# A mixture of experts with a ring of row buffers: freeing a buffer once its rows are turned, weights through another queue, and no store of empty rows

## What is computed

```python
logits = xt @ wg
probs = softmax(logits); idx = argmax(probs)
mask = one_hot(idx, E); locations = cumsum(mask, axis=0) - mask
mask = mask * (locations < C)                       # C = T // E = 512 places per expert, E = 8
exp_out = einsum("ech,efh->ecf", exp_in, W) + b[:, None, :]
x = x + 0.5 * gate * exp_out_of_the_token
```

## Time and profile before

| | |
|---|---|
| median of three runs | 1435.03 us (1433.06 to 1435.62) |
| the profiled execution | 1434.59 us |
| its span, first to last instruction | 1433.3 us |
| mean granted clock of TensorE | 0.911 of full speed |
| busy: PE, DVE, ACT, POOL | 1115.5, 943.4, 827.8, 319.2 us |
| r = 0, first indirect DMA of results starts | 87.33 us |
| r = 1, first indirect DMA of results starts | 947.45 us |

### The profile page before, as it was taken

How to read it: one execution, slowest core, us unless ns; L and a number is a source line. 1 busy time by engine, 2 the same in 40 slices (tenths; PEclk the granted TensorE clock), 3 DMA queues, 4 the chain that set the end, 5 groups by cost and what they waited for, 6 DMA issues and landing times. The chain is left out here.

```text
span 1433.3 us, 30188 instructions
## 1 busy us (share of the span) xinstructions
PE 1115.5 (78%) x12280; PEld 908.0 (63%) x12280; DVE 943.4 (66%) x1619; ACT 827.8 (58%) x964; POOL 319.2 (22%) x375
## 2 busy tenths in 40 slices
PE   6265589889999899989889996555639965984797
PEld 3144476568888887548888884244318963642697
DVE  5111665789999984678999997313845545764365
ACT  7211444589999952378999995523623325653332
POOL 4744001000000000100000000755262430337244
PEclk9688699999999999999999998878779986987799
DMA  9866400411221200011121212265433432003343
GB/s 255 294 210 206 141 1 0 156 64 65 86 91 61 90 2 1 0 63 61 64 88 65 87 61 89 101 201 181 139 124 100 120 119 92 1 12 127 86 123 101
DMA packets 84588, 140.61 MB, mean 98 GB/s; under 512 B 10574, under 2 KB 71246, under 8 KB 79950
## 3 DMA queue, kind: packets, MB, share of 16 engines
q1 hardware_dynamic: 70276, 102.15, 22.3%
q0 software_dynamic: 13056, 35.87, 7.0%
q10 hardware_dynamic: 1120, 0.66, 0.2%
HBM read 86.62 MB, written 56.27 MB: 100 GB/s over the span
## 5 line engine op out<-in xcount | busy, mean ns | idle before, releaser
L1390 ACT ACTIVATE b_signs<-b_q_everywhere,normed 128x2048 bf16<-128x2048 f32 x224 | 429.2, 1990 | 24.5 <-PE banks L1277 23.3
L1277 PE MATMUL banks<-b_value_parts,b_signs 128*128 128x102 bf16 x8192 | 392.7, 208 | 40.4 <-DVE b_signs L1565 37.9
L1277 PEld LDWEIGHTS banks<-b_value_parts,b_signs 128*128 128x128 bf16 x8192 | 375.9, 97 | 60.1 <-DVE b_signs L1565 49.9
L1565 DVE TENSOR_SCALAR b_signs<-b_q_everywhere,normed 128x2048 bf16<-128x2048 f32 x288 | 350.5, 1275 | 8.3 <-PE banks L1277 8.3
L684 POOL DMA_INDIRECT moe_slots<-normed,slot_of_token x128 | 124.9, 976 | 39.1 <-issue 33.5
L1617 POOL MEMSET b_value_parts<- 128x256 bf16 x2 | 2.6, 1324 | 450.2 <-PE banks L1150 450.2
L438 PE MATMUL banks<-identity,normed 128*128 128x128 f32 x256 | 49.3, 326 | 48.6 <-ACT normed L373 48.4
L346 DVE BATCH_NORM_STATS2 ln_stats<-residual 128x6 f32<-128x256 f32 x192 | 71.3, 416 | 18.0 <-SPq L1809 10.6
L449 PE MATMUL banks<-normed_T,wg 128*8 128x256 f32 x256 | 72.7, 410 | 1.7 <-ACT normed_T L547 1.7
L373 ACT ACTIVATE normed<-residual,ln_shift,ln_rstd 128x256 f32<-128x256 f32 x128 | 68.1, 587 | 3.7 <-DVE ln_shift L368 3.7
L438 PEld LDWEIGHTS banks<-identity,normed 128*128 128x128 f32 x256 | 32.1, 162 | 59.1 <-ACT normed L373 42.9
(11 more groups left out here) (279 smaller groups left out, 2358.9 us busy)
## 6 DMA issues: line engine op xcount, KB each, us to landing
b_q_everywhere<-q_rows SPq DMA_DIRECT2D x32, 1024.0 KB, 4.8
normed<-expert_rows SPq DMA_DIRECT2D x6, 1024.0 KB, 10.2
d_rows<-moe_slots SPq DMA_DIRECT2D x40, 129.5 KB, 2.2
f_rows<-moe_slots SPq DMA_DIRECT2D x40, 129.5 KB, 2.2
moe_slots<-a_empty SPq DMA_DIRECT2D x8, 518.0 KB, 9.2
a_rows<-moe_slots SPq DMA_DIRECT2D x16, 259.0 KB, 3.9
moe_empty_slots<-a_empty SPq DMA_DIRECT2D x8, 518.0 KB, 5.4
moe_slots<-moe_empty_slots SPq DMA_DIRECT2D x1, 4144.0 KB
```

The lines of the kernel that those rows point to most:

```text
L1277: ins = nc.tensor.matmul(banks[qt // QPB][:, qt % QPB * VP:(qt % QPB + 1) * VP], t.SG[:, (hh * TB + kt) % RING, qt * P:(qt + 1) * P], t.VO ...
L1390: nc.scalar.activation(t.SG[:, g % RING, :], t.QB[:, hh % 2, :], ACT.Sign, bias=t.NKT[:, kt, hh % H:hh % H + 1]).then_inc(s.sign_a, 1)
L1565: nc.vector.tensor_scalar(t.SG[:, g % RING, :], t.QB[:, hh % 2, :], t.KTM[:, kt, hh % H:hh % H + 1], 2.0, ALU.is_gt, ALU.mult).then_inc(s. ...
```

## The change

- Row numbers: POOL copies the two columns of row numbers of pair j into a table of their own, `ROW`, as soon as the pair is loaded, three pairs ahead of the results (`xs_row`). The indirect DMAs read their row numbers there. SP reloads a row buffer when PE has turned it (`xs_turned`) and POOL has copied its numbers, no longer when the results have landed.
- The second kind's weights and bias pieces are issued by ACT, in steps 0, 2, 5 and 8 of its loop (`act_weights_in`), each with a semaphore of its own.
- `moe_empty_slots` and its eight stores are gone. POOL makes a small table of spare row numbers (`NUMBER`, 128 x 32 x 3) ahead of `EMPTY`, and in attention SP writes, in eight DMAs, only the three last columns of each row of `moe_slots` from it (`sp_empty`). The store of 1036 KB moves ahead of the row loads.

```diff
+def sp_empty(k):
+    for e in range(E):
+        k.nc.sync.dma_start(tiles_of(k.by_slot[e])[:, :, D:RW],
+                            k.NUMBER[:, e * CAP // P:(e + 1) * CAP // P, :].bitcast(F32)).then_inc(k.s.slots_empty, 16)
...
             if j >= RING_X:
-                nc.sync.wait_ge(back[(j - RING_X) % 3], back_count(r, j - RING_X))
+                nc.sync.wait_ge(s.xs_turned, r * pairs + j - RING_X + 1)
+                nc.sync.wait_ge(s.xs_row, r * pairs + j - RING_X + 1)
...
-        if r == 0 and n >= 0 and n % 2:
-            cut = slice(n // 2 * NT * 2 // pairs, (n // 2 + 1) * NT * 2 // pairs)
-            nc.sync.dma_start(tiles_of(k.empty0)[:, cut, :], t.EMPTY[:, cut, :]).then_inc(s.empty_stored, 16)
...
+        if r == 1 and n in (0, 2, 5, 8):
+            act_weights_in(k, (0, 2, 5, 8).index(n))
...
-    for n in range(pairs):
-        nc.gpsimd.wait_ge(xs_in[n % RING_X], xs_count(r, n))
-        nc.gpsimd.wait_ge(s.ys, at + n + 1)
-        pool_rows_back(k, t, n, k.y_rows)
+    for n in range(-3, pairs):
+        if n + 3 < pairs:
+            j = n + 3
+            nc.gpsimd.wait_ge(xs_in[j % RING_X], xs_count(r, j))
+            nc.gpsimd.tensor_copy(t.ROW[:, j, :], t.XS[:, j % RING_X, :, D].bitcast(I32)).then_inc(s.xs_row, 1)
+        if n >= 0:
+            nc.gpsimd.wait_ge(s.xs_row, at + n + 1)
+            nc.gpsimd.wait_ge(s.ys, at + n + 1)
+            pool_rows_back(k, t, n, k.y_rows, [t.ROW[:, n, i:i + 1] for i in range(2)])
...
-            nc.sync.dma_start(k.by_slot, k.empty0.rearrange("(e r) d -> e r d", e=E)).then_inc(s.slots_empty, 16)
+            nc.sync.wait_ge(s.numbers_made, 1)
+            sp_empty(k)
...
+    k.ps.step(nc.gpsimd.memset(k.NUMBER[:, :, :], 0))
+    io(k.NUMBER[:, :, 0], [[P, NT]], T, 1).then_inc(s.numbers_made, 1)
     EMPTY = k.top0[0].EMPTY
```

More of the change, by code:

```diff
@@ L186, in plan @@
     k.EPS = m.take("eps", [P, 2])
+    k.NUMBER = m.take("empty_slots_rows", [P, NT, RW - D], I32)
     k.REV = m.take("rank_of_expert", [P, E])
@@ L225, in plan_moe0 @@
     t.YS = m.take("expert_out", [P, 3, 2, D])
+    t.ROW = m.take("row_numbers", [P, NJ0 // 2, 2], I32)
     t.EMPTY = m.take("empty", [P, NT, RW]) if first else None
@@ L700, in sp_moe0 @@
         nc.sync.dma_start(tiles_of(k.y_rows[0:T, :]), t.EMPTY[:, :, 0:D]).then_inc(s.y0_zeroed, 16)
+        nc.sync.dma_start(tiles_of(k.slots1[SPARE:SPARE + (NJ1 - NT) * P, :]), t.EMPTY[:, E:E + NJ1 - NT, :]).then_inc(s.spares_stored, 16)
         for n in range(2):
@@ L705, in sp_moe0 @@
     xs_in = (s.xs_in0, s.xs_in1, s.xs_in2, s.xs_in3, s.xs_in4)
-    back = (s.back0, s.back1, s.back2)
     pairs = NJ0 // 2
@@ L813, in act_moe0, with act_weights_in @@
             nc.scalar.activation(k.B_PARTS[:, :], k.B_RAW[:, :], ACT.Copy).then_inc(s.bparts, 1)
+def act_weights_in(k, piece):
+    nc, s = k.nc, k.s
+    layer, c = divmod(piece, KD)
+    nc.scalar.dma_start(k.w_raw[layer, c].rearrange("p (e f) -> p e f", e=E),
+                        k.a["w1" if layer == 0 else "w2"][:, c * P:(c + 1) * P, :].rearrange("e p f -> p e f")).then_inc(
+                            (s.raw_in0, s.raw_in1, s.raw_in2, s.raw_in3)[piece], 16)
+    if c == 0:
+        nc.scalar.wait_ge(s.bparts_zero, 1)
+        nc.scalar.dma_start(k.B_RAW[3 * layer:3 * layer + 3, :], k.bias_parts[layer]).then_inc(s.bparts_in, 16)
 def dve_moe0(k, r):
@@ L863, in pool_rows_back @@
         nc.gpsimd.indirect_dma_start(
-            out=to, out_offset=bass.IndirectOffsetOnAxis(ap=t.XS[:, n % RING_X, i, D:D + 1].bitcast(I32), axis=0),
+            out=to, out_offset=bass.IndirectOffsetOnAxis(ap=row[i], axis=0),
             in_=t.YS[:, n % 3, i, :], in_offset=None).then_inc(back[n % 3], 16)
@@ L1026, in pool_moe1 @@
         nc.gpsimd.wait_ge(s.m_ys, at + n + 1)
-        pool_rows_back(k, t, n, k.out if m else k.y_rows)
+        pool_rows_back(k, t, n, k.out if m else k.y_rows, [t.XS[:, n % RING_X, i, D:D + 1].bitcast(I32) for i in range(2)])
 def sp_attention(k):
```

33 lines of the change are left out of this document (11 added, 22 removed).

## The result

The changed kernel takes **1422.05 us** (median of four runs, 1418.19 to 1423.42); the kernel before took 1435.32 us in the same comparison (1433.06 to 1439.42). The ratio is 0.990, with a 95% interval of 0.9869 to 0.9931. The prediction was 1423.8 us, faster.

What follows compares the result with a forecast made beforehand. With the circle of waits through the row buffers opened, POOL's own pace was taken as the bound: -8.8 - 2.6 + 0.2 = -11.2 us, from 1434.59 to 1423.4, plus 0.44 for the median, 1423.8 us; range 1420.3 to 1430.9.

Steps and rivals of the forecast that it cites:

- The circle: Placing results, r = 0: row loads wait for landed results, so POOL waits 10.9 us, which go; 6.0 in r = 1.
- POOL as what is late next: Result placing: with the circle open, POOL's pace bounds; r = 0 takes 42.1 us, -8.8 us.
- Copies: POOL's new copies of row numbers between indirect DMAs: 0.16 us each, 13 of them, 2.1 us (0 to 4.2).
- The start: Ahead of the scatter: POOL's new fill and list come before `EMPTY`; between 0 and 0.5 us, taken as +0.2.
- Stretches in r = 1: Indirect DMAs starting beside DVE's four remainders of the weights lose 1.65 us each, 6.6 in all (4.1 to 9.2).
- The rival that took from this that nothing is stretched: r = 1: DVE's remainder does not hold POOL; r = 1 falls to 42.4 us, the time to 1417.2 us; 3%.
- r = 1 as a sum: Result placing in r = 1: 40.3 pace + 2.1 copies + 6.6 stretches = 49.0 us, -2.6 us (-7.2 to +2.1).
- The ring of three result buffers: Result placing: binds only from a landing of 5.3 us; as a rival, at 6.0 us landing, 1428.4 us; 8%.
- Weights through ACT: The second kind's weight loads: six issues, 4.6 us, hide in ACT's wait for PE; effect nothing.
- The small pieces: Refill in attention: 4096 pieces of 12 bytes, 0 to 18 us, hidden; rival at 200 ns each, 1449.3 us, 6%.

Runs made afterwards that it cites:

- the table alone: The kernel before with only the table of row numbers and the early freeing of row buffers; 1425.29 us, ratio 0.9937.
- the third part alone: The kernel before with only the small refill, no stores of empty rows and the 1036 KB store moved ahead; 1426.76 us, ratio 0.9950.
- The PSUM version: The changed kernel with DVE's remainder reading the rounded copy from PSUM, in halves; 1424.72 us, ratio 0.9897; with four result buffers too, 1418.86 us, ratio 0.9854.
- the change's second run: The changed kernel measured once more without an edit, in the third comparison; 1427.37 us, ratio 0.9907.

## Why the prediction was right, and where not

**The circle, and POOL as what is late next: right as a sum, too simple as a cause in r = 0.** The prediction gave all 10.9 us of waits to the circle through the row buffers and nothing to the eight stores, "since waits already hold their effect". The sum is right because the change does both. But the table alone leaves 4.4 us of waits, 4.0 of them in the ring of result buffers, and the third part alone, without the stores, takes 6.7 us off r = 0. So the sum does not show that its cause was right, and in part it is luck: had the change been the table alone, the step would have been 3.2 us too good (-8.8 against -5.6).

**Copies: 0.16 predicted, 0.06 measured.** 12 of them stand between DMAs, not 13: 0.7 us in place of 2.1. With this and the start r = 0 came out at -9.4 (rows back at 130.34 against 139.72) where -8.8 + 0.2 was predicted.

**The start: 0.2 predicted.** The new table on POOL cost nothing there: the scatter's first copy starts at 32.48 against 32.45. The first results come 0.6 us later, and not for that reason. Busy time of the engines in a stretch after the scatter (PE, PEld, DVE, ACT, POOL; then granted clock, DMA share, GB/s) of the changed kernel:

```profile
84.00:86.00 2.00, 2.00 (x7) 1.55 (x6) 0.00 (x0) 0.00 (x0) 0.00 (x0) 0.51 0.68 207
```

PE has been idle until 80.9 us and runs at the lower level (0.50, 1.2 GHz) until almost 86; before, the same stretch was granted 0.76 on average. The clock rose later. That the change moved it isn't shown: in the profiled executions above the first indirect DMA of results starts between 87.33 and 92.18 us, in the changed kernel itself at 87.93 and at 90.33.

**Stretches in r = 1: 4 x 1.65 = 6.6 predicted, 5.7 and 6.3 measured**, each in four places, one or two of them on a copy, which the prediction did not have. The PSUM version takes away the two SBUF operands and with them all four, and the short sum at 1048.69 shows that length is not the reason, so the cause is shown. A stretched DMA ends 0.84 us after the remainder, as the prediction's own row had it, so it loses what is left of the remainder at its start less 0.13: 2.28 - 0.62 - 0.13 = 1.53 for the DMA at 947.90. The whole 2.29, the prediction's upper bound, can't be lost by that. The Trainium skill ("SBUF — State Buffer", Who interferes with whom) says that a VectorE instruction with at most one SBUF input, outside the 2-port modes, leaves GpSimd alone; the 0.97 us beside L855 agrees. The Trainium skill says there too that one with two SBUF inputs contends with a GpSimd instruction that reads SBUF, and infers that descriptor writing goes on beside it. The held copies, which read SBUF, agree with the first; and the traces don't contradict the inference, since the DMA at 973.43 was not held by a remainder that began after it. What is held at a DMA's start no run shows. The rival that took from this that nothing is stretched, 1417.2 us, fell.

**r = 1 as a sum.** The predicted 49.0 us lie between the measured 48.0 and 50.1, but not because the terms were right: copies took 0.7 in place of 2.1, stretches 5.7 and 6.3 in place of 6.6, and waits, put at nothing, 1.3 and 2.7. The misses offset each other, which is luck.

**The ring of three result buffers.** The prediction let it bind from a landing of 5.3 us. It held a median against that, and a median doesn't tell of the long landings. The ring binds in the table alone at a median of 4.4, where the longest landing in the profile is 5.9, and a little in r = 1 (1.3 and 2.7 us) at a median of 3.0, where the longest is 6.9; in the change's second run, too, 6.9 us passed from an indirect DMA's start until the sum that waits for its landing. In the changed kernel's r = 0 it does not bind.

**Weights through ACT: nothing**, as predicted; weights back on SP give the same time.

**The small pieces:** predicted at 0 to 71 ns, about 27.5 and at most 31 measured; the refill's 256 pieces per engine are down 5.94 + 2.9 = 8.8 us after the first issue, of the 25.7 there were. The Trainium skill ("DMA: Bandwidth & Descriptors", Specifications) has pieces under 512 bytes read, modified and written; whether these were, no run here shows, but their price is below what the prediction took from that page.

## What to carry to other kernels

A buffer should be held by the data that is still needed, not by the row numbers that lie beside it: copying 2 numbers a row cost 0.06 us a pair and opened a circle of waits. When one ring is opened, the next one (here the result buffers) and the traffic that lengthens its landings decide how much of the gain comes through, so try the parts one by one. And where POOL issues DMAs back to back, look at what DVE does beside it: a sum of two SBUF operands that took 2.28 us cost 1.1 to 2.1 us each time that POOL issued or copied behind its start; with one operand in PSUM it cost nothing.

## What the runs showed of the hardware that was not expected

- DVE's sum of two SBUF operands holds a plain POOL copy too: 1.85 to 1.87 us in place of 0.19 in the changed kernel.
- It holds an indirect DMA only at its start: one that starts behind the sum ends 0.84 us after it, one already running (973.43) keeps its 0.97 us. A sum of 0.49 us is enough for that (1.25 us).
- A POOL copy between two indirect DMAs costs 0.06 us, a second one 0.12.
- Taking stores out of r = 0 that nothing in the stretch waits for (eight dropped, one of 1036 KB moved ahead) made it 6.7 us shorter, as the landings and loads beside them took less.
- One kernel's length of r = 1 varied by 2 us between executions (48.0 and 50.1), with the same program, by how its landings and stretches fell.
